# The values of the 8-head attention in the rotating plain PSUM banks, with a new timetable

## What is computed

```
def _L2_conv_ref(x, norm_w, norm_b, qkv_w, qkv_b, proj_w, proj_b):
    ...
    hid = _group_norm(xr, norm_w, norm_b)
    qkv = jnp.einsum('oc,bcl->bol', qkv_w, hid) + qkv_b[None, :, None]
    ...
    weight = jnp.einsum('bhct,bhcs->bhts', q * scale, k * scale)
    weight = jax.nn.softmax(weight.astype(jnp.float32), axis=-1).astype(weight.dtype)
    a = jnp.einsum('bhts,bhcs->bhct', weight, v)
    h = a.reshape(b, c, L)
    h = jnp.einsum('oc,bcl->bol', proj_w, h) + proj_b[None, :, None]
    ...
    return (x + h) / RESCALE
```

## Time and profile before

| | before |
|---|---|
| median of three runs | 2128.81 us (2125.54 to 2136.21) |
| span of the profiled execution | 2132.0 us |
| PE, ACT, DVE, POOL busy over the span | 94%, 88%, 87%, 62% |

### The profile page before, as it was taken

One profiled execution on the slowest core, in us unless ns is written; L12 is line 12 of the kernel. 1 busy time (PEld: TensorE's weight loads), 2 busy tenths in 40 slices (PEclk: granted clock), 3 DMA queues, 4 the chain that ended last, 5 costly groups with the idle time before them and its releaser, 6 DMA issues.

```text
span 2132.0 us, 60375 instructions
## 1 busy us (share of the span) xinstructions
PE 2014.2 (94%) x15232; PEld 1692.3 (79%) x15232; DVE 1851.5 (87%) x4683; ACT 1883.5 (88%) x6231; POOL 1313.0 (62%) x2954
## 2 busy tenths in 40 slices
PE   5578999999999999999999999999999999999977
PEld 3367788888888888888888888888888888888766
DVE  6778999999999999999999999999999999997532
ACT  2258999999999999999999999999999999999984
POOL 3554667676666767676676666666667666664321
PEclk8699999999999999999999999999999999999988
DMA  3000011011001101110110011011001101000000
GB/s 128 15 24 9 32 40 40 17 38 38 31 29 38 38 15 38 38 38 23 38 38 24 29 38 38 23 38 38 30 23 38 38 23 38 31 32 18 23 24 38
DMA packets 29823, 70.34 MB, mean 33 GB/s; under 512 B 6252, under 2 KB 7088, under 8 KB 29744
## 3 DMA queue, kind: packets, MB, share of 16 engines
q1 hardware_dynamic: 26928, 67.68, 9.1%
q10 hardware_dynamic: 2816, 1.72, 0.3%
HBM read 30.85 MB, written 12.85 MB: 20 GB/s over the span
## 4 chain that ended last, share of the span: by engine, by line
PE 80%; DVE 8%; ACT 5%; issue 4%; POOL 2%; SPq 1%; DVEq 1%; DMA 0%; POOLq 0%; ACTq 0%
PE ps_e L1176 19%; PE ps_c L1176 19%; PE ps_b L1176 15%; PE ps_a L1176 10%; PE ps_s L1176 9%; PE ps_s L1231 6%; DVE y L1168 3%; DVE y L1149 1%; ACT e L839 1%; PE ps_a L1478 1%; DVE x L1088 1%; ACT e L831 1%; DVE m L1113 1%; DVE y L1163 1%; ACT pt L845 1%
## 5 line engine op out<-in xcount | busy, mean ns | idle before, releaser
L831 ACT ACTIVATE e<-ps_s,nm 98x196 f32<-98x196 f32 x1024 | 426.5, 447 | 44.4 <-DVE nm L967 43.2
L839 ACT ACTIVATE e<-e,rden 98x196 f32<-98x196 f32 x1024 | 408.4, 477 | 1.1 <-DVE rden L1072 1.0
L596 POOL TENSOR_SCALAR xn<-x,gn_scale,gn_shift 128x196 f32<-128x196 f32 x384 | 308.3, 813 | 20.8 <-POOL gn_shift L591 20.8
L1168 DVE SCALAR_TENSOR_TENSOR y<-opad,w_dw,y 128x406 f32<-128x406 f32 x512 | 313.4, 664 | 0.0
L1149 DVE SCALAR_TENSOR_TENSOR y<-xpad,w_dw,y 128x406 f32<-128x406 f32 x512 | 300.8, 641 | 0.0
L967 DVE TENSOR_REDUCE nm<-ps_s 98x4 f32<-98x784 f32 x256 | 239.5, 967 | 34.8 <-PE ps_s L1176 34.8
L845 ACT COPY pt<-ps_s 98x392 f32<-98x392 f32 x512 | 237.2, 509 | 7.6 <-PE ps_s L1231 4.1
L1231 PE MATMUL ps_s<-w_eye,e 98*98 98x98 f32 x2048 | 229.1, 250 | 8.5 <-ACT e L839 8.2
L831 ACT ACTIVATION_READ_ACCUMULATOR e<-ps_s,nm 98x1 f32 x1024 | 233.6, 228 | 0.0
L1231 PEld LDWEIGHTS ps_s<-w_eye,e 98*98 98x98 f32 x2048 | 201.1, 130 | 39.5 <-issue 23.5
L574 POOL TENSOR_TENSOR gn_t<-gn_group 128x4 f32<-128x4 f32 x96 | 26.6, 277 | 312.5 <-DVE gn_group L1017 222.7
(11 more groups left out here) (227 smaller groups left out, 5569.6 us busy)
## 6 DMA issues: line engine op xcount, KB each, us to landing
x_in<-in_x SPq DMA_DIRECT2D x32, 392.0 KB, 3.3
x_res<-in_x SPq DMA_DIRECT2D x32, 392.0 KB, 3.2
x2b<-x SPq DMA_DIRECT2D x32, 392.0 KB, 2.7
out<-x SPq DMA_DIRECT2D x32, 392.0 KB, 2.6
out_pairs<-out SPq DMA_DIRECT2D x32, 392.0 KB, 2.5
w_q<-in_q SPq DMA_DIRECT2D x3, 256.0 KB
w_k<-in_k SPq DMA_DIRECT2D x3, 256.0 KB
w_v<-in_v SPq DMA_DIRECT2D x3, 256.0 KB
```

The costliest lines, as they stand in the source:

```text
L596: g.tensor_scalar(dst[:, c, of_image(i)], src[:, c, of_image(i)], t.scale[:, j:j + 1], t.shift[:, j:j + 1], ALU.mult, ALU.add).then_inc(t. ...
L831: s.activation(e2[:, j, tc], tile(use)[0:HALF, of_image(tc)], ACT.Exp, bias=nm2[:, j, tc:tc + 1], accum_out=den2[:, 2 * i + tc, h:h + 1]). ...
L839: s.activation(e2[:, j, tc], e2[:, j, tc], ACT.Copy, scale=rden2[:, 2 * i + tc, h:h + 1]).then_inc(p2_done[j].sem, 1)
L1168: v.scalar_tensor_tensor(out=dst, in0=window(opad, c, k, CR), scalar=tap, in1=dst, op0=ALU.mult, op1=ALU.add).then_inc(conv2_steps.sem, 1)
```

## The change

`av0` to `av3` leave the first score bank: av0, av1 and av3 go to bank a, av2 to bank b. The plain banks' other items are dealt out anew, and the tables of PE, ACT and DVE have new numbers throughout; those of POOL change in two places that keep their order, SP's are as before. The computation and the instructions are the same; their order in three queues and the banks' turns are not.

On PE the order from the scores of group 0 to the second block's products becomes: gn1, sc0, t0_1, av3, o0_1, o0_0, hv0, s3_1, hq1, hk1, proj1, tn0_0, tn0_1, hv1, tn0_3, tn0_2, proj0, sc1, av0, kv0, kv1. Before it was: gn1, v0, t0_0, t0_1, sc0, s3_0, o0_1, o0_0, hv1, av3, hv0, s3_1, tn0_1, hq1, tn0_0, tn0_2, proj1, tn0_3, hk1, proj0, sc1, kv0, kv1, av0. Around group 2 it becomes ctx0, ctx1, q0_0, t3_1, sc2, av1, out1, out0, k0, pw0, o3_1 (before: ctx0, ctx1, sc2, q0_0, t3_1, out0, out1, av1, o3_1). On DVE max0_0 now stands ahead of gn1's copy, before it stood behind. On ACT high1_0 stands directly ahead of hk1, and tn0_0, tn0_3, tn0_2, high1_1, s3_1, hv1 and av0 behind that.

The diff, cut to what is spoken of:

```diff
 PE_AT = {
-    "q0_1": 102, "q0_0": 115, "k0": 133, "s0_0": 144, "s0_1": 153, "v0": 176, "t0_0": 178, "t0_1": 180, "o0_1": 185,
-    "o0_0": 187, "pw0": 254, "pw1": 268, "mlp0": 283, "mlp1": 284, "gn1": 302, "kv0": 340, "kv1": 342, "kv2": 346,
-    "kv3": 349, "q1_0": 353, "q1_1": 356, "ctx0": 365, "ctx1": 367, "out0": 374, "out1": 376, "gn2": 385, "hk0": 425,
-    "hq0": 429, "sc0": 438, "hv1": 445, "hv0": 448, "tn0_1": 452, "hq1": 454, "tn0_0": 456, "tn0_2": 457,
-    "tn0_3": 461, "hk1": 463, "sc1": 466, "av0": 472, "tn1_1": 483, "tn1_3": 488, "tn1_0": 490, "tn1_2": 492,
-    "sc2": 497, "av1": 506, "tn2_1": 512, "tn2_2": 515, "tn2_3": 519, "tn2_0": 521, "sc3": 526, "av2": 533,
-    "tn3_1": 548, "tn3_0": 549, "tn3_2": 551, "tn3_3": 555, "av3": 575, "proj1": 587, "proj0": 593, "gn3": 607,
-    "q3_1": 658, "v3_1": 659, "v3_2": 663, "q3_0": 670, "v3_0": 672, "v3_3": 674, "s3_0": 695, "s3_1": 706,
-    "t3_0": 731, "t3_1": 757, "o3_1": 764, "o3_0": 778,
+    "q0_1": 99, "q0_0": 117, "k0": 128, "s0_0": 156, "s0_1": 161, "v0": 171, "t0_0": 176, "t0_1": 193, "o0_1": 195,
+    "o0_0": 196, "pw0": 259, "pw1": 267, "mlp1": 297, "mlp0": 298, "gn1": 319, "kv0": 345, "kv1": 346, "kv2": 347,
+    "kv3": 349, "q1_0": 353, "q1_1": 354, "ctx0": 367, "ctx1": 368, "out1": 382, "out0": 383, "gn2": 392, "hk0": 428,
+    "hq0": 429, "sc0": 448, "hv0": 453, "hq1": 455, "hk1": 456, "tn0_0": 458, "tn0_1": 459, "hv1": 460, "tn0_3": 461,
+    "tn0_2": 468, "sc1": 470, "av0": 471, "tn1_1": 479, "tn1_0": 480, "tn1_3": 484, "tn1_2": 493, "sc2": 506,
+    "av1": 509, "tn2_0": 521, "tn2_2": 524, "tn2_1": 525, "tn2_3": 526, "sc3": 534, "av2": 548, "tn3_0": 561,
+    "tn3_2": 564, "tn3_1": 565, "tn3_3": 570, "av3": 578, "proj1": 585, "proj0": 597, "gn3": 606, "v3_2": 650,
+    "v3_1": 659, "v3_3": 667, "v3_0": 669, "q3_1": 671, "q3_0": 687, "s3_0": 702, "s3_1": 710, "t3_0": 732,
+    "t3_1": 761, "o3_1": 774, "o3_0": 775,
...
 ACT_AT = {
...
-    "high1_0": 336, "high1_1": 340, "kv0": 350, "kv1": 358, "kv2": 359, "keys0": 360, "keys1": 361, "kv3": 363,
...
-    "hk0": 435, "hq0": 439, "sc0_0": 444, "sc0_1": 445, "sc0_2": 448, "sc0_3": 450, "less0_1": 454, "less0_0": 455,
-    "hv1": 456, "less0_2": 457, "tn0_1": 459, "less0_3": 460, "hq1": 461, "tn0_0": 462, "tn0_3": 465, "tn0_2": 466,
-    "hk1": 467, "hv0": 470, "sc1_0": 473, "sc1_1": 475, "sc1_2": 476, "sc1_3": 477, "less1_0": 481, "less1_1": 482,
-    "av0": 483, "less1_3": 484, "less1_2": 492, "tn1_3": 494, "tn1_1": 499, "tn1_2": 500, "tn1_0": 502, "sc2_1": 508,
...
+    "high1_0": 332, "high1_1": 340, "kv0": 354, "kv1": 355, "keys0": 357, "kv2": 358, "kv3": 361, "keys1": 362,
...
+    "hk0": 432, "hq0": 434, "sc0_0": 444, "sc0_1": 446, "sc0_2": 449, "sc0_3": 450, "less0_0": 452, "hv0": 453,
+    "hq1": 454, "less0_1": 455, "less0_3": 456, "less0_2": 458, "tn0_1": 459, "hk1": 461, "tn0_0": 462, "tn0_3": 464,
+    "tn0_2": 467, "hv1": 470, "av0": 473, "sc1_0": 474, "sc1_1": 475, "sc1_3": 477, "sc1_2": 478, "less1_1": 479,
...
 DVE_AT = {
...
-    "conv2_1": 201, "conv2_2": 232, "conv2_3": 237, "conv2_4": 238, "conv2_5": 243, "conv2_6": 245, "conv2_7": 249,
-    "conv2_8": 252, "pw0": 260, "pw1": 274, "act0_low0": 279, "act0_low1": 284, "mlp0": 290, "mlp1": 296,
-    "stats1": 299, "gn1": 301, "low1_0": 330, "low1_1": 334, "kv0": 338, "kv1": 340, "kv2": 346, "rk0": 349,
...
-    "out1": 384, "stats2": 387, "gn2": 390, "low2_0": 423, "low2_1": 426, "max0_0": 433, "max0_1": 435,
-    "rden0_0": 443, "rden0_1": 448, "max1_0": 463, "max1_1": 465, "rden1_0": 469, "rden1_1": 472, "av0": 483,
...
+    "conv1_7": 62, "conv1_8": 65, "s0_0": 153, "s0_1": 161, "sum0_0": 164, "sum0_1": 171, "conv2_0": 191,
...
+    "stats1": 300, "gn1": 304, "low1_0": 326, "low1_1": 327, "kv0": 349, "kv1": 351, "kv2": 355, "rk0": 356,
...
+    "out0": 384, "stats2": 387, "gn2": 395, "low2_0": 419, "low2_1": 421, "max0_0": 431, "max0_1": 439,
+    "rden0_0": 443, "rden0_1": 445, "max1_0": 467, "max1_1": 469, "av0": 475, "rden1_0": 476, "rden1_1": 478,
...
 BANK_USES = {
-    "a": ("t0_1", "o0_1", "gn1", "ctx0", "hv0", "gn3", "v3_2", "v3_0", "t3_0", "t3_1", "o3_1",),
-    "b": ("k0", "v0", "o0_0", "mlp0", "q1_0", "ctx1", "out1", "v3_1", "v3_3", "s3_1",),
-    "c": ("q0_0", "s0_0", "pw0", "kv1", "kv3", "q1_1", "hq0", "hq1", "hk1", "q3_0", "s3_0", "o3_0",),
-    "e": ("q0_1", "s0_1", "t0_0", "pw1", "mlp1", "kv0", "kv2", "out0", "gn2", "hk0", "hv1", "proj1",
-          "proj0", "q3_1",),
+    "a": ("k0", "s0_0", "t0_0", "mlp0", "ctx0", "hv0", "av0", "av1", "av3", "proj1", "t3_0", "o3_1",),
+    "b": ("q0_0", "o0_1", "pw0", "gn1", "kv2", "q1_0", "hq0", "av2", "v3_2", "v3_3", "s3_1",),
+    "c": ("mlp1", "kv1", "q1_1", "ctx1", "out0", "hk0", "hk1", "proj0", "gn3", "q3_1", "s3_0", "o3_0",),
+    "e": ("q0_1", "s0_1", "v0", "t0_1", "o0_0", "pw1", "kv0", "kv3", "out1", "gn2", "hq1", "hv1", "v3_1", "v3_0",
+          "q3_0", "t3_1",),
 }
...
@@ -291,7 +291,7 @@
         bank_s = [Bank(f"bank_s{j}", ps_s[:, j], [
             use for g in range(GROUPS) for use in (
                 (f"sc{g}_{j}", PE_AT[f"sc{g}"], 2), (f"tn{g}_{j}", PE_AT[f"tn{g}_{j}"], 1),
-                *([(f"av{g}", PE_AT[f"av{g}"], 1)] if j == 0 else []))]) for j in range(HG)]
+)]) for j in range(HG)]
```

## The result

| | before | after |
|---|---|---|
| median, same chip | 2129.57 us (4 runs) | 2196.89 us (2191.22 to 2197.24, 4 runs) |
| ratio | 1 | 1.0305, 95% interval 1.0281 to 1.0328 |
| span of the profiled execution | 2132.0 us | 2194.7 us |
| period of the loop | 61.92 us | 63.55 us |

The change makes the kernel 67 us slower; the forecast was 12 us faster. The period is worked out from TensorE's rows as in the prediction: the distance from the first matmul of a block to the first of the next, its median over the periods between 480 and 1700 us, summed over all blocks. The starts of gn1 on POOL show where the 62.7 us between the two spans lie: the first comes at 84.9 us in either, the fourth 11.1 us later (269.0 against 257.9 us), the next two periods are 65.6 and 65.8 us against 61.3 and 61.6 (8.5 us), and nearly all of the rest is 1.63 us in each further period.

A forecast was written before the change was run, and what follows sets the result against it. TensorE was taken to set the loop's pace, with ACT and DVE close behind. The terms, -1.07 + 0.15 + 0.5 = -0.42 us a period, over 28 periods gave 12 us less, a median of 2117 us, range 2094 to 2165.

The forecast's parts named there:

- What bounds the kernel: Whole loop: TensorE sets the pace, ACT and DVE close behind, so a badly put step can stop it within a period.
- What goes away: TensorE's waits at kv0 (0.6) and sc2 (0.15) and two joints (0.32) go: 1.07 us a period in all.
- kv0's part: The wait of kv0 for DVE's read of proj0 in bank e goes: 0.6 us a period.
- The joints: Scores directly before values on TensorE save one entering (0.09) and one leaving (0.07): 0.32 us a period for two.
- hv0: hv0 on TensorE waits for the reads of av3 in bank a: 0.15 us added, 0 to 0.4.
- o3_1: o3_1 in bank a behind k0: a wait of 0 to 0.5 us, taken as 0.
- gn1 and proj0: gn1's later copy delays POOL's norm, ACT's high1_0 and the read of hk1: proj0 waits 0.5 us a period.
- second rival: POOL's norm as slow as gn2's 10.3 us: proj0 waits 1.3, +0.38 a period, 2139 us; chance 0.22.
- third rival: POOL's stall beside DVE's convolution steps stays: proj0 waits 3.4, +2.5 us a period, 2198 us; chance 0.15.
- An order with a wait that I haven't seen: Rival, shared with joints and bank giving nothing: an unseen wait in the order, 2120 to 2150 us; chance 0.05.
- The ramps: Filling and draining: TensorE saturated in some 26 of 32 periods, ramps have part of the gain, so 28 periods counted.

The follow-up runs named there:

- gn1's copy first: The changed kernel with DVE's copy of gn1 put ahead of max0_0 again: 2163.36 us, ratio 1.0139 to the kernel before.
- high1_0 later: The changed kernel with ACT's high1_0 put behind its copies of hk1 and the three remaining tn0 blocks: 2187.03 us, ratio 1.0255 to the kernel before.

## Why the prediction was wrong

**What bounds the kernel** was right: TensorE's order sets the pace, and a step put badly in ACT's or DVE's queue stops it.

**What goes away.** 1.07 us a period was taken; the trace shows 0.68 + 0.19 + 0.32 = 1.19 gone. But kv0's part is worth 0.44 where it is taken out alone: the step asked what is late next for kv0 and named hv1's bank, and in the order before it was an operand, low1_1, 0.24 us behind. In the changed order it is hv1's bank as soon as proj0 is on time (kv0 starts 0.053 behind its reader).

**The joints** were right: 0.09 and 0.07 each. The rule cited there (the Trainium skill, TensorEngine Tiling (Array Packing), Key Properties: TensorE drains whenever the tiling mode changes) would, at the price that the prediction gave it, have kept the entering from row to column strips. No such price is in the rows: it is 254 ns from the last scores' matmul to the next block's first, whether values or a plain block follow, and the values take 0.80 as where they stand apart. They don't speak against a drain itself: the later fours of matmuls within the scores follow one another after 141 to 146 ns.

**hv0** was right: 0.12 measured (0.15, 0 to 0.4), at 0.06 behind DVE's read of av3. o3_1 too (0 to 0.02).

**gn1 and proj0**: the mechanism was right in each link, and one term was missized. POOL's start (S+1.42 against S+1.46), the stall that goes (0.23 us where 3.09 stood) and TensorE's arrival (some S+11.9 against S+11.7) came out as written. POOL's length did not: 10.36 against 9.56. Of the 0.80, half lies in the small instructions (8.65 us to the first xn against 8.26 without the stall; six behind the first two took 0.41 to 0.47, where most take 0.20), half in the first two xn (1.71 against 1.30), all beside steps of the convolution on DVE. That is the second rival's 10.3, and proj0's wait of 1.04 idle and 1.26 by distance is its 1.3. The rival had stood at 0.22 and the forecast at 0.40, though the row that both were measured against, gn2's 10.3, was the nearest one there was; taking 9.56 meant that all else stays as fast while the norm moves beside other work of DVE.

**The step that failed** is the one that is not there. With proj0 at 1.26 the sum gives the second rival's 2139, not 2197. (That the third rival had 2198 is chance: its stall isn't there, and proj0 waits 1.26, not 3.4.) The prediction priced the new places of the values, gn1 and o3_1, and passed over the sentence in the change that the plain banks' other items are dealt out anew. 44 of 47 old tenants got a new tenant before them, and the order on three queues moved readers and operands away from their blocks. Beside proj0 and hv0 eight further waits stand there, 1.6 us a period that the sum put at nothing: 0.76 at plain banks, 0.60 at scores behind ACT's copies, 0.26 at an operand. With proj0's wait all but gone the period is still 0.9 over that of before. "An order with a wait that I haven't seen" was given a chance of 0.05 and 2150 us at most. The holds could have been added up before: every bank's former tenant and its reader's end stand in the trace, and the new order of blocks is in the table. What that sum can't give beforehand is the readers' lateness after the change, which made 23 of the 38 us.

**The ramps.** 28 effective periods were assumed; the 1.63 us come in nearly all of them, and filling and the first two periods cost 20 us more. With gn1's copy first the fourth gn1 starts at 260.3 us and the next two periods are 62.7 and 62.6, so most of this comes from the same late norm.

**What stays open.** Why the other 0.9 us a period are where they are is shown for single waits only: they move on when one is taken out, and no dealing of the banks that was found mends them. That the full banks (27% against 11%) cause them was argued, not shown, and the waits at the scores and at hk0 (0.86) are for other things than a plain bank; a kernel of the changed order with more room in the banks wasn't tried. Nor was the late copy of gn1 put into the order before, where it can't stand behind max0_0: t0_1, ahead of sc0, needs gn1's bank.

## What to carry to other kernels

In a saturated loop with a strict order, price every block's distance to its bank's former reader and to its operands, not only those of the blocks that are moved; a sum of the holds per bank and the share of time in which all banks are held is a first estimate of the room that a new tenant finds (that it foretells the loss wasn't shown here). Taking out one wait is worth the distance to the next thing that is late for the same block, its operands as well as its bank, and here that was between nothing and four fifths of the wait. When a small instruction on a slow engine stands ahead of a faster engine's queue, look first at what its first input stands behind.

## What the runs showed of the hardware

- The same norm of POOL took 12.46, 10.36 and 11.36 us to its second xn in three orders of DVE's work. Its 128x4 instructions take 0.20 us, or up to 0.60, and once in a norm 1.82 or 3.09, and the long one isn't the same line in each (L577, L587): a stall that is moved away from one instruction can meet another. (The Trainium skill, SBUF - State Buffer, Who interferes with whom, has DVE and POOL share ports under a lock; the rows agree in kind.) In both cases the long one began beside a maximum on DVE and ended 0.08 or 0.09 us behind the last of the convolution steps that stood back to back behind that maximum, four before and two with gn1's copy first. Two cases make no rule, but the order of DVE's table shows such places.
- A wait can cost more than its idle time: in q0_1, behind q1_1 in either trace, the first matmul took 429 ns where it waited and 329 where it didn't. But a first matmul is also longer without a wait: proj0 behind tn0_2 took 264 ns where nothing held it (high1_0 later) and 285 where it waited, against 180 for its others. So compare it with the same pair of blocks unhindered.
- Where a bank's reader is what releases a block, the block's first matmul starts 53 to 56 ns behind the reader's end; kv0 before, and hv0, kv3 and proj0 after, are within that, which makes it a mark by which such waits are found.
